# Row maxima of two heads in one VectorE operation out of two PSUM banks, in a fused attention and expert layer

## What is computed

```python
qh = q.reshape(B, S, H, D)
kh = k.reshape(B, S, H, D)
qk = jnp.einsum('bthd,bshd->bhts', qh, kh)
causal = jnp.tril(jnp.ones((S, S), dtype=bool))
qk = jnp.where(causal, qk, -jnp.inf)
attn = jax.nn.softmax(qk, axis=-1)
vh = v.reshape(B, S, D, H)
qkv = jnp.einsum('bsdh,bhts->bthd', vh, attn)
```

## Time and profile before

| | |
|---|---|
| median of three executions | 857.16 us |
| the profiled execution, its own time | 856.38 us |
| span of the profile, first to last instruction | 854.6 us |
| mean granted clock of TensorE | 0.987 of full |
| TensorE matmul busy | 780.8 us (91%) |
| ScalarE busy | 581.7 us (68%) |
| VectorE busy | 554.1 us (65%) |
| GpSimd busy | 184.0 us (22%) |

### The profile page before, as it was taken

How to read it: one execution, slowest core, us unless ns; L and a number is a source line. 1 busy time by engine, 2 the same in 40 slices (tenths; PEclk the granted TensorE clock), 3 DMA queues, 4 the chain that set the end, 5 groups by cost and what they waited for, 6 DMA issues and landing times.

```text
span 854.6 us, 27793 instructions
## 1 busy us (share of the span) xinstructions
PE 780.8 (91%) x11935; PEld 361.9 (42%) x11935; DVE 554.1 (65%) x1207; ACT 581.7 (68%) x683; POOL 184.0 (22%) x356
## 2 busy tenths in 40 slices
PE   1478999999999999999999989999999899999994
PEld 1243334443444444444444444443444443444443
DVE  6877334777776767766677777667677777321216
ACT  1257787776767787788777767666666577666572
POOL 4453112101121102111211021100210721223222
PEclk9999999998999999999999999999999999999997
DMA  3112332005130002000300030000400102200003
GB/s 107 58 60 78 125 101 79 3 2 105 42 113 3 3 3 73 2 3 2 114 3 3 2 113 2 2 3 2 150 3 2 46 7 75 61 13 17 17 19 99
DMA packets 29375, 36.64 MB, mean 43 GB/s; under 512 B 6190, under 2 KB 24014, under 8 KB 28998
## 3 DMA queue, kind: packets, MB, share of 16 engines
q1 hardware_dynamic: 27862, 32.03, 12.8%
q0 software_dynamic: 1248, 2.57, 0.9%
q10 hardware_dynamic: 144, 0.27, 0.1%
HBM read 24.25 MB, written 10.24 MB: 40 GB/s over the span
## 4 chain that ended last, share of the span: by engine, by line
PE 76%; DVE 13%; ACT 5%; issue 4%; DMA 0%; POOL 0%; POOLq 0%; ACTq 0%; DVEq 0%
PE PS L973 24%; PE PS L953 23%; PE PS L919 13%; DVE MP L1284 5%; ACT PR L856 4%; PE PS L998 3%; PE PS L982 2%; PE PS L1015 2%; PE PS L923 2%; PE PS L1038 1%; DVE OT L1305 1%; PE PS L997 1%; PE PS L891 1%; DVE KA L1214 1%; PE PS L1006 1%
## 5 line engine op out<-in xcount | busy, mean ns | idle before, releaser
L856 ACT ACTIVATE PR<-PS 128x1024 f32<-128x1024 f32 (+1 forms) x576 | 530.9, 975 | 159.3 <-PE PS L953 157.3
L1284 DVE TENSOR_REDUCE MP<-PS 128x1 f32<-128x512 f32 (+3 forms) x640 | 373.5, 608 | 124.9 <-PE PS L919 69.3
L953 PE MATMUL PS<-QA,KA 74*32 74x512 bf16 (+3 forms) x5120 | 333.6, 351 | 8.1 <-ACT PR L856 7.4
L973 PE MATMUL PS<-PR,VA 128*32 128x512 f32 (+3 forms) x2560 | 287.8, 533 | 3.8 <-DVE OT L1305 2.6
L919 PE MATMUL PS<-KA,QA 72*32 72x512 bf16 (+3 forms) x2560 | 229.5, 352 | 13.3 <-DVE MP L1284 10.9
L676 POOL TENSOR_SCALAR_AFFINE_SELECT PR<-PR 128x256 f32<-128x256 f32 x256 | 102.2, 416 | 481.8 <-ACT PR L856 476.0
L953 PEld LDWEIGHTS PS<-QA,KA 74*32 74x32 bf16 x5120 | 118.2, 97 | 156.2 <-ACT PR L856 68.2
L919 PEld LDWEIGHTS PS<-KA,QA 72*32 72x32 bf16 x2560 | 69.2, 95 | 119.2 <-DVE MP L1284 79.7
L973 PEld LDWEIGHTS PS<-PR,VA 128*32 128x32 f32 x2560 | 73.4, 110 | 51.4 <-issue 13.4
L923 PE MATMUL PS<-CM,IDB 128*32 128x128 bf16 x1024 | 57.7, 220 | 0.0
L1425 DVE SCALAR_TENSOR_TENSOR FC<-FC,PS 128x256 f32<-128x256 f32 x23 | 9.7, 421 | 61.8 <-ACT FC L839 61.8
(11 more groups left out here) (177 smaller groups left out, 408.4 us busy)
## 6 DMA issues: line engine op xcount, KB each, us to landing
QA<-q_parts SPq DMA_DIRECT2D x96, 96.0 KB
KA<-k_parts SPq DMA_DIRECT2D x48, 96.0 KB
QA<-in_W SPq DMA_DIRECT2D x1, 2048.0 KB, 7.5
q_parts<-QA SPq DMA_DIRECT2D x4, 384.0 KB, 2.6
q_parts<-KA SPq DMA_DIRECT2D x4, 384.0 KB, 2.5
expert_tokens<-ZERO SPq DMA_DIRECT2D x1, 1483.5 KB, 12.7
QA<-expert_tokens SPq DMA_DIRECT2D x1, 1483.5 KB, 7.3
KA<-k_shared SPq DMA_DIRECT2D x48, 24.0 KB
```

What stands on the lines that cost most here:

```text
L856: act.activation(PR[:, (2 * n + p) % RING, :, 0:w], PS[:, 2 * p:2 * p + 2, 0:w], ACT.Exp)\
L953: last = pe.matmul(PS[r:r + STRIP, hh, start:start + CH - q0], KA[0:ROWS, b, kb // BPC, 0 if ffn else hh, key:key + STRIP], QA[0:ROWS, b, ...
L973: last = pe.matmul(PS[32 * hh:32 * hh + 32, 6, q0:CH], VA[:, slot % 2, kb, hh, :], PR[:, (2 * n + hh // 2) % RING, hh % 2, start:start + C ...
L1284: dve.reduce_max(MP[:, BPC * (HG * (qb // BPC) + hh) + qb % BPC, kc:kc + 1], PS[:, 4 + u % 2, 0:item_width(item)], AX).then_inc(s_mr, 1)
```

## The change

VectorE reduces two heads in one operation. A unit is now an item of a *pair* of heads (320 units). TensorE fills bank 4 with the first head of the pair and bank 5 with the second, and signals once; VectorE reads both banks in one operation of 2 x w elements a partition and writes two columns. Before each of the two fills TensorE waits until the unit before has been reduced. The units of a step stand in two places, dealt out by halves of a step: after scores 0, and after values and turn. None stands between scores 1 and values. Matmuls, masks and the results are the same; 320 reductions fewer are issued.

```diff
-UNITS = len(ITEMS) * HG
+UNITS = len(ITEMS) * 2
...
         for n in range(first, end):
-            own += width(SEQ[n][1]) + 400
-            if n in HOLD:
-                continue
-            while u < UNITS and (n == end - 1 or done * total < own * work):
-                out[n].append((a, u // HG, u % HG))
-                done += item_width(u // HG) + 64
-                u += 1
+            for half in range(2):
+                own += 0.5 * (width(SEQ[n][1]) + 400)
+                if n in HOLD:
+                    continue
+                while u < UNITS and (n == end - 1 and half or done * total < own * work):
+                    out[n][half].append((a, u // 2, u % 2))
+                    done += item_width(u // 2) + 64
+                    u += 1
...
 def maxima_at(n):
-    u = MAXIMA[n] if n < N else []
-    x = (len(u) + 2) // 3
-    y = x + (len(u) + 1) // 3
-    return u[:x], u[x:y], u[y:]
+    return MAXIMA[n] if n < N else ([], [])
...
             def max_unit(unit):
-                a, item, hh = unit
+                a, item, pair = unit
...
-                bank = PS[:, 4 + u % 2, :]
...
-                free(("unit", u))
-                for r in range(0, P, STRIP):
+                for k in range(2):
+                    bank, hh = PS[:, 4 + k, :], 2 * pair + k
+                    free(("unit", u, k))
                     for r in range(0, P, STRIP):
...
                 last.then_inc(s_mm, 1)
...
                 for p in range(2):
                     if n < N:
                         scores(n, p)
-                    for unit in parts[p]:
-                        max_unit(unit)
+                    if p == 0:
+                        for unit in parts[0]:
+                            max_unit(unit)
                 if 0 <= n - LAG < N:
                     values(n - LAG)
                 if ended(n - LAG - 1) is not None:
                     turn(ended(n - LAG - 1))
-                for unit in parts[2]:
+                for unit in parts[1]:
                     max_unit(unit)
...
-                dve.reduce_max(MP[:, BPC * (HG * (qb // BPC) + hh) + qb % BPC, kc:kc + 1],
-                               PS[:, 4 + u % 2, 0:item_width(item)], AX).then_inc(s_mr, 1)
+                dve.wait_ge(s_mm, unit_number(unit) + 1)
+                m = HG * (qb // BPC) + 2 * pair
+                heads = MP[:, BPC * m:BPC * (m + 2), kc].rearrange("p (k t) -> p k t", k=2)
+                dve.reduce_max(heads[:, :, qb % BPC], PS[:, 4:6, 0:item_width(item)], AX).then_inc(s_mr, 1)
```

More of the change, by code:

```diff
@@ L118, in spread_maxima @@
 def spread_maxima():
-    out = [[] for _ in range(N)]
+    out = [([], []) for _ in range(N)]
     for a, (first, end) in enumerate(MAX_SPAN):
         total = sum(width(SEQ[n][1]) + 400 for n in range(first, end))
-        work = HG * sum(item_width(i) + 64 for i in range(len(ITEMS)))
+        work = 2 * sum(item_width(i) + 64 for i in range(len(ITEMS)))
         u = done = own = 0
         for n in range(first, end):
-            own += width(SEQ[n][1]) + 400
-            if n in HOLD:
-                continue
-            while u < UNITS and (n == end - 1 or done * total < own * work):
-                out[n].append((a, u // HG, u % HG))
-                done += item_width(u // HG) + 64
-                u += 1
+            for half in range(2):
[6 more added lines that the diff above has]
+                    u += 1
     return out
@@ L139, in unit_number @@
 def unit_number(unit):
-    a, item, hh = unit
-    return UNITS * a + HG * item + hh
+    a, item, pair = unit
+    return UNITS * a + 2 * item + pair
 def maxima_at(n):
-    u = MAXIMA[n] if n < N else []
-    x = (len(u) + 2) // 3
-    y = x + (len(u) + 1) // 3
-    return u[:x], u[x:y], u[y:]
+    return MAXIMA[n] if n < N else ([], [])
 def maxima_end(a, c):
-    return max(n for n in range(N) for u in MAXIMA[n] if u[0] == a and ITEMS[u[1]][0] // BPC == c)
+    return max(n for n in range(N) for u in MAXIMA[n][0] + MAXIMA[n][1] if u[0] == a and ITEMS[u[1]][0] // BPC == c)
 FRONT_AT = {0: [("Q", 1), ("K", 1)], 1: [("P", 4), ("P", 5)], 2: [("X", 3)], 5: [("Q", 2), ("K", 2)],
@@ L200, in bank_uses @@
         parts = maxima_at(n)
[L201 to L206, removed]
+        for half in range(2):
+            if half and ended(n - LAG - 1) is not None:
+                out.append((("turn", ended(n - LAG - 1)), 7, "D"))
+            for u in parts[half]:
+                for k in range(2):
+                    out.append((("unit", unit_number(u), k), 4 + k, "M"))
         for name, k in works(n):
@@ L912, in max_unit @@
                 w = item_width(item)
-                bank = PS[:, 4 + u % 2, :]
-                if hh == 0 and qb % BPC == 0 and kc == 0:
+                if pair == 0 and qb % BPC == 0 and kc == 0:
                     loaded(SLOT_OF[a], c)
-                free(("unit", u))
-                for r in range(0, P, STRIP):
[L918 to L921, removed]
-                    for r in range(0, P, STRIP):
-                        last = pe.matmul(bank[r:r + STRIP, w - P:w], IDB[:, r:r + STRIP], CM[:, :],
-                                         start=False, stop=True)
+                for k in range(2):
+                    bank, hh = PS[:, 4 + k, :], 2 * pair + k
+                    free(("unit", u, k))
+                    for r in range(0, P, STRIP):
+                        q = qb % BPC * P + r
+                        last = pe.matmul(bank[r:r + STRIP, 0:w], QA[0:STACK, b, c, hh, q:q + STRIP],
+                                         KA[0:STACK, b, kc, hh, 0:w], start=True, stop=not diag)
+                    if diag:
+                        for r in range(0, P, STRIP):
+                            last = pe.matmul(bank[r:r + STRIP, w - P:w], IDB[:, r:r + STRIP], CM[:, :],
+                                             start=False, stop=True)
                 last.then_inc(s_mm, 1)
@@ L1279, in max_unit @@
             def max_unit(unit):
-                a, item, hh = unit
+                a, item, pair = unit
                 qb, kc = ITEMS[item]
-                u = unit_number(unit)
-                dve.wait_ge(s_mm, u + 1)
-                dve.reduce_max(MP[:, BPC * (HG * (qb // BPC) + hh) + qb % BPC, kc:kc + 1],
-                               PS[:, 4 + u % 2, 0:item_width(item)], AX).then_inc(s_mr, 1)
+                dve.wait_ge(s_mm, unit_number(unit) + 1)
+                m = HG * (qb // BPC) + 2 * pair
+                heads = MP[:, BPC * m:BPC * (m + 2), kc].rearrange("p (k t) -> p k t", k=2)
+                dve.reduce_max(heads[:, :, qb % BPC], PS[:, 4:6, 0:item_width(item)], AX).then_inc(s_mr, 1)
             def shift_parts(k):
@@ L1289, in shift_parts @@
                 m = HG * BPC
-                last = UNITS * a + HG * max(i for i in range(len(ITEMS)) if ITEMS[i][0] // BPC == c) + HG
+                last = UNITS * a + 2 * max(i for i in range(len(ITEMS)) if ITEMS[i][0] // BPC == c) + 2
                 dve.wait_ge(s_mr, last)
@@ L1476, in _ @@
                 parts = maxima_at(n)
-                for unit in (*parts[0], *parts[1]):
+                for unit in parts[0]:
                     max_unit(unit)
```

## The result

| | before | after |
|---|---|---|
| median of the runs, us | 858.17 (854.01 to 859.2, 4 runs) | 939.48 (937.15 to 950.18, 4 runs) |
| ratio over all runs | | 1.098 (95% interval 1.089 to 1.107); the medians alone give 1.095 |
| the profiled execution, us | 856.38 | 939.75 |
| its span, us | 854.6 | 938.0 |
| mean granted clock of TensorE | 0.987 | 0.966 |

What follows compares the result with a forecast made beforehand. TensorE was taken to bound steps 34 to 256: 93 us of new waits, less 13 removed, plus 1 for delayed second reductions and 3 for the clock, make +84 on 856.38 us: 940 us, range 925 to 960 (8 in 10: 915 to 975).

Steps and rivals of the forecast that it cites:

- TensorE bounds the stretch, and VectorE's saving is worth nothing: Steps 34 to 256: TensorE has no gap, so the 49 us freed on VectorE by halving the reductions bring nothing.
- The round trip of 1.94 us: From one double fill's start to the next possible one at 512 wide: fill, VectorE's start, 1.227 us operation, release.
- The three kinds of places, 93 us: Added TensorE waits: second place to next step's first 65 us, first to second place 10, several in one place 18.
- The lower bound: Two-bank reduction as quick as ScalarE's 1022 ns operation: round trip 1.73 us at 512, sum of waits about 71 us.
- What was removed, 13 us: TensorE's old waits for reductions, 24 places, 15 us at most with hidden parts; about 2 us in step 58 stays.
- The clock, +3 us: TensorE's idle pieces grow, so one or two more clock falls were allowed, at 1.7 to 3.3 us each.
- The signs: Profile after: two-bank reduction 1.2 us, VectorE's sum on it about 325, wait before fills about 70, long wait 0.9.
- The clock rival: Waits in successive full steps pull TensorE's clock to its lower level: 26 us more, 966 us; chance 0.20.
- the eight pairs of steps: Successive steps starting at 34, 43, 53, 157, 170, 174, 189, 210, where the clock rival expected falls of 3.3 us each.
- The quick reduction: Rival: the two-bank reduction streams as ScalarE does, waits sum to 71 us, time 918 (905 to 925); chance 0.11.
- Waits hidden by ScalarE: Rival: exponentials set the pace, so TensorE's waits fall into time it waits anyway; no change, 857 us; chance 0.03.
- A limit on VectorE: Rival: VectorE was the real limit, so the 13 us go and no new wait shows; 843 us, chance 0.04.

Runs made afterwards that it cites:

- without run-ahead: The kernel before, with one wait added: TensorE fills a bank only when the unit before it, in the other bank, has been reduced; 1202.43 us, one run.
- the short read: The changed kernel with the double reduction reading only 64 columns of each bank; 872.24 us, one run, -3.6 us against before on its chip.
- the evenly dealt units: The changed kernel with its double units dealt to three places of a step, as far apart as they go; 928.56 us, 1.061 against before.
- one by one: The changed kernel with its order of fills kept, but each head signalled, reduced and released by itself (640 reductions); 907.98 us, 1.040 against before.

## Why the prediction was right, step by step

*TensorE bounds the stretch, and VectorE's saving is worth nothing.* Right, though "without a gap" was read from one full window: from 100 to 700 us TensorE was busy for 578 of 600 us. By the durations of its single rows the reductions took 640 x 608 ns = 389 us before and 320 x 1065 ns = 341 after, 48 us less where 49 were forecast. The busy time fell by 32.6 us only (373.5 to 340.9), since reductions that follow each other without a wait overlap a little in the rows of before, and none do after. None of it reached the time.

*The round trip of 1.94 us.* Right to the rows' last digit: 184.33 to 186.27.

*The three kinds of places, 93 us.* The measured time without a stream is 98.7 us over the whole stretch. By stage the sum is 29, 13, 25 and 27 us, and the measured time 31, 15, 26 and 28. The stages grew by less, 27.5, 12.6, 17.9 and 22.0, since waits of the kernel before went (next item). The forecast list of places was good to 6%; the experiments put the same sum to five further tests, within 4 us each but for the one without run-ahead, which it missed by 21. The lower bound took its 1022 ns from ScalarE's operation over two other banks, not "the same" ones; the 1226 ns leave the bound unused.

*What was removed, 13 us.* Mis-sized. The waits before were 24.2 us without a stream in 92 places, not 15 at most: I had added the hidden 0.17 us only to the 24 waits that the earlier trace rows shows, and not to those short enough to be hidden altogether. So the net of the waits is 98.7 - 24.2 = 74.5 us, where 93 - 13 = 80 was forecast. Some of the 24.2 are other delays of VectorE and are still there after.

*The clock, +3 us.* Mis-sized too. In the stretch the clock stood at the lower level for 27.2 us after and 10.2 before. The 17 us more, in which TensorE was busy nearly throughout, cost at most half, 8.5 us. With the 74.5 they cover the 80.0, with 3 us to spare. So the clock took some 5 to 8 us, more than allowed. That the total came out within 1 us of the forecast is in part luck: the two misses, 5.5 us too many for waits and 2 to 5 too few for the clock, nearly cancelled. One of the falls, by windows (length, then busy time of PE, PEld, DVE, ACT, POOL, then the granted clock):

```profile
213.00:216.00 3.00, 0.89 (x20) 0.33 (x16) 2.75 (x5) 1.12 (x2) 0.00 (x0) 1.00 0.01 3
216.00:219.00 3.00, 2.80 (x44) 1.24 (x47) 0.97 (x2) 1.02 (x1) 0.00 (x0) 0.51 0.46 131
```

TensorE was busy for 0.89 of 3.00 us, and then the clock halved. This is the place that gave the fall of the earlier trace rows at 197 us: VectorE has five other operations in front of the reduction, and the wait for it, 1.36 us in the earlier trace rows, is 2.11 us now. Another fall is new and comes from the waits of the change alone, where narrow units stand two in a place:

```profile
156.07 0.24 PE L918 MATMUL PS<-KA,QA 72*32 72x128 bf16 x4 [0.89 <-DVE MP L1285]
...
157.02 0.24 PE L918 MATMUL PS<-KA,QA 72*32 72x128 bf16 x4 [0.53 <-DVE MP L1285]
```

```profile
155.00:158.00 3.00, 1.57 (x48) 0.83 (x48) 1.87 (x3) 1.11 (x3) 0.41 (x1) 1.00 0.02 5
158.00:162.00 4.00, 3.62 (x41) 1.40 (x37) 1.41 (x2) 1.81 (x2) 0.41 (x1) 0.51 0.00 0
```

*The signs.* The wait before fills was to reach about 70 us and is 72.9, 71.0 of them for reductions; the long wait 0.9 us is there. "About 325 us" for VectorE's sum is a slip: by the prediction's own durations it is 224 x 1.227 + 32 x (0.958 + 0.690 + 0.421) = 341 us, and 340.9 was measured. Over steps 34 to 256 the granted clock is 0.98, so that sign of being wrong did not come.

*The rivals.* The clock rival's mechanism exists (the kernel without run-ahead has it at full size: 55 us in 170 steps), and in the changed kernel it is there in small: five falls in the stretch in place of two, but none after the waits at the eight pairs of steps that the rival named (one, at 653.0 us, comes in step 210, the first of such a pair, ahead of its waits). The page "TensorE: Matmul & The Clock Gate" of the Trainium skill ("A second HAM failure mode: psum-queue depth-cycling") says that in a kernel which cycles through PSUM banks small idle pieces between groups of matmuls, if frequent enough, make the clock swing. The runs agree for 380 of them in 659 us and hardly for 128 in 485 us. The quick reduction is out by the 1226 ns. Waits hidden by ScalarE are out, since its own idle time grew by 72.6 us. A limit on VectorE is out by the short read: with the same number of instructions and 64 columns the kernel only gets back to the time before.

*Where numbers came from another chip.* The forecast of a difference held on both chips, +81 and +82. The expectations that named absolute times were reckoned from the first chip: 909, 893 and 869 us agree with the measured 908, 896 and 872 only because the chip's 17 us and an overestimate of the difference by 14 to 19 us cancel. In the fourth, 918 for the evenly dealt units, the overestimate was 7 us and 929 was measured. Part of the overestimate is the clock, which these sums leave out: in steps 34 to 203 it stood at the lower level for 17.1 us in the changed kernel and for 0, 3.4 and 0 us in the first three of these.

## What to carry to other kernels

One operation that reads two PSUM banks turns two buffers into one: count the round trip from fill to fill (fill, start of the reader, its length, release) against the work that the filling engine has in between, place by place. If the filling engine is the bound, an instruction saved on the reader is worth nothing and each missing microsecond is paid in full. Where several small pieces fit into one bank, one operation over all of them saves the same fixed cost and keeps the second bank: here -2.2% in place of +9.3%, on one and the same chip.

## What the runs showed of the hardware that was not expected

- A reduction to two or four outputs runs on the same line as one to a single output: 692 and 691 ns for 512 elements into 2 and 4 columns, 689 ns into one; 1226 ns for 1024 elements over two banks.
- On two chips ScalarE and VectorE stand still, for 11.8 and 10.8 us in the trace of the kernel before, while GpSimd issues indirect DMAs, and TensorE starts one to four matmuls at a time, mostly 0.7 us or more apart; on the first chip the same program issues them as fast (one each 1.26 us) without it. The kernel before is 2% slower on those chips, and 16.2 us of the difference lie in the steps around this place.
- TensorE's clock fell much more often than its waits grew in number. In steps 34 to 203, 380 waits of 0.51 us in the mean (no run-ahead) went with 18 falls and 133 us at the 1.2 GHz level, 128 waits of 0.55 us (the changed kernel) with 2 falls and 17 us, and 146 waits of 0.28 us (one by one) with none.
